# Adding the second key block's exponentials onto the first's on GpSimd, in the first attention of a four-stage kernel

## The reference, cut to what matters

```python
q = layernorm(x)                      # 16 heads of 32; keys and values are both ctx
scores = einsum('bhqd,bhkd->bhqk', q, k) * 32 ** -0.5   # causal: key <= query
exp_c  = exp(scores - rowmax(scores))
new_s  = exp_c.sum(axis=-1)
out    = einsum('bhqk,bhkd->bhqd', exp_c / new_s, v)
x      = x + tanh(g_xattn[0]) * out
```

## Time and profile before

| | |
|---|---|
| median of 3 runs | 1129.12 us (1126.06 to 1130.04) |
| profiled execution, its own time | 1127.54 us |
| its span, first to last instruction | 1125.5 us |
| PE / DVE / ACT / POOL busy, share of the span | 97% / 75% / 50% / 10% |
| POOL instructions | 212 |
| a turn of L0, PE start to PE start | 33.05 us |

### The profile page before, as it was taken

How to read it: one execution, slowest core, us unless ns; L and a number is a source line. 1 busy time by engine, 2 the same in 40 slices (tenths; PEclk the granted TensorE clock), 3 DMA queues, 4 the chain that set the end, 5 groups by cost and what they waited for, 6 DMA issues and landing times.

```text
span 1125.5 us, 25576 instructions
## 1 busy us (share of the span) xinstructions
PE 1092.2 (97%) x10386; PEld 662.7 (59%) x10386; DVE 839.0 (75%) x1437; ACT 567.1 (50%) x918; POOL 117.9 (10%) x212
## 2 busy tenths in 40 slices
PE   8899999999999999999999999899999999999998
PEld 3555555556777777777776655455554545454544
DVE  5788888778676657567566667887878788778786
ACT  4767666765433333333333353464554546372654
POOL 1101100110000000000001212020202030111010
PEclk9999999999999999999999999999999999999899
DMA  9565555433112011021010200101010101000001
GB/s 362 194 194 181 187 189 177 145 105 122 67 39 66 20 39 38 23 73 39 19 57 20 85 10 30 38 2 57 1 57 1 58 1 39 1 11 10 11 10 39
DMA packets 29267, 79.24 MB, mean 70 GB/s; under 512 B 3040, under 2 KB 3296, under 8 KB 28896
## 3 DMA queue, kind: packets, MB, share of 16 engines
q1 hardware_dynamic: 29152, 77.61, 21.0%
HBM read 65.02 MB, written 12.58 MB: 69 GB/s over the span
## 4 chain that ended last, share of the span: by engine, by line
PE 89%; DVE 4%; issue 3%; ACT 2%; POOL 1%; DMA 1%; SPq 0%; DVEq 0%; ACTq 0%; POOLq 0%
PE bank L693 10%; PE bank L589 10%; PE bank L590 10%; PE bank L675 10%; PE bank L551 9%; PE bank L798 8%; PE bank L431 5%; PE bank L828 5%; PE bank L786 5%; PE bank L748 3%; PE bank L767 2%; PE bank L456 2%; PE bank L516 2%; PE bank L483 2%; PE bank L504 2%
## 5 line engine op out<-in xcount | busy, mean ns | idle before, releaser
L589 PE MATMUL bank<-ARENA,W 128*128 128x256 f16 x1024 | 227.3, 273 | 0.7 <-issue 0.7
L590 PE MATMUL bank<-ARENA,W 128*128 128x256 f16 x1024 | 227.3, 273 | 0.0
L1006 ACT ACTIVATE ARENA<-bank 128x512 f32<-128x512 f32 (+3 forms) x143 | 92.9, 687 | 72.3 <-PE bank L431 35.5
L675 PE MATMUL bank<-W,ARENA 128*128 128x512 bf16 x512 | 120.8, 379 | 0.0
L551 PE MATMUL bank<-ARENA 128*128 128x512 f32 x256 | 117.7, 603 | 0.9 <-DMA ARENA<-in_wkv 0.9
L798 PE MATMUL bank<-W,ARENA 128*128 128x512 bf16 x512 | 117.7, 379 | 0.4 <-DVE W L1737 0.4
L693 PE MATMUL bank<-ARENA 128*128 128x512 f32 x256 | 116.9, 599 | 0.0
L589 PEld LDWEIGHTS bank<-ARENA,W 128*128 128x128 bf16 x1024 | 100.2, 98 | 19.1 <-issue 1.3
L590 PEld LDWEIGHTS bank<-ARENA,W 128*128 128x128 bf16 x1024 | 100.2, 98 | 18.0
L1006 ACT ACTIVATE ARENA<-ARENA 128x512 f16<-128x512 f32 x64 | 40.3, 630 | 133.3 <-DVE ARENA L1591 129.5
L1591 DVE SCALAR_TENSOR_TENSOR ARENA<-bank,ARENA 128x512 f32<-128x512 f32 x64 | 48.0, 750 | 72.3 <-PE bank L590 69.0
(11 more groups left out here) (181 smaller groups left out, 1799.6 us busy)
## 6 DMA issues: line engine op xcount, KB each, us to landing
W<-in_w SPq DMA_DIRECT2D x48, 512.0 KB, 4.3
ARENA<-in_w SPq DMA_DIRECT2D x24, 512.0 KB, 3.6
kv_store<-ARENA SPq DMA_DIRECT2D x32, 256.0 KB, 4.3
W<-kv_store SPq DMA_DIRECT2D x15, 512.0 KB, 4.1
ARENA<-in_ctxT SPq DMA_DIRECT2D x8, 512.0 KB, 3.9
X<-in_x SPq DMA_DIRECT2D x8, 512.0 KB, 5.7
ARENA<-in_ctx SPq DMA_DIRECT2D x8, 512.0 KB, 5.9
out<-X SPq DMA_DIRECT2D x16, 256.0 KB, 2.1
```

What stands on the lines that cost most here:

```text
L589: pe.matmul(bank[:, i * S:(i + 1) * S], W0[:, at:at + P], xt_half(b, 0)[:, k, :], start=(k == 0), stop=False)
L590: mm = pe.matmul(bank[:, i * S:(i + 1) * S], W0[:, at:at + P], xt_half(b, 1)[:, k, :], start=False, stop=(k == KD - 1))
L675: mm = pe.matmul(banks[6 + t], hx(q, what)[:, i * S + t * P:i * S + (t + 1) * P], W0[:, UP_AT + m * D:UP_AT + (m + 1) * D], start=(m == 0 ...
L1006: return act.activation(to, src, ACT.Copy)
```

## The change

GpSimd adds, for each group of four heads, the second key block's exponentials onto the columns of the first block that belong to the same queries (`a_add_probs`). The sums then need the first block alone, over 256 columns. The weighing keeps both blocks; since the first block's columns now hold p0 + p1, the second block is multiplied by v1 - v0, which GpSimd makes in place once per batch (`a_values_apart`): v0 (p0 + p1) + (v1 - v0) p1 = v0 p0 + v1 p1. Weigh and sum wait for these two through new semaphores `a_pa` and `a_dv`. For half 0 they are cut in two parts by head group, and the second parts stand behind scores(b,3).

```diff
-                pe.wait_ge((s.ld_rv0, s.ld_rv1)[b % 2], 16 * (b // 2 + 1))
-                pe.wait_ge(s.a_ex, 16 * b + 8 * half + 8)
-                for n in range(2):
+                if parts[0] == 0:
+                    pe.wait_ge(*ringA[4].freed(f"pv{half}", turn))
+                    pe.wait_ge(s.a_dv, b + 1)
+                for n in parts:
+                    pe.wait_ge(s.a_pa, 4 * b + 2 * half + n + 1)
...
-                for n in range(2):
-                    for kb in range(TB):
-                        at, q0 = kb * S, kb * P
-                        for j in range(4):
-                            mm = pe.matmul(part(total, j)[:, q0:S], bufA["count"][:, n, :], bufA["PT"][:, 4 * n + j, at:at + S - q0],
-                                           start=(kb == 0 and n == 0), stop=(kb == 1 and n == 1), skip_group_check=True)
-                mm.then_inc(s.a_sum, 1)
...
+                for n in parts:
+                    pe.wait_ge(s.a_pa, 4 * b + 2 * half + n + 1)
+                    for j in range(4):
+                        mm = pe.matmul(part(total, j)[:, 0:S], bufA["count"][:, n, :], bufA["PT"][:, 4 * n + j, 0:S],
+                                       start=(n == 0), stop=(n == 1), skip_group_check=True)
...
-                a_weigh(turn, b, 0)
+                a_weigh(turn, b, 0, (0,))
+                a_sum(turn, b, 0, (0,))
                 a_scores(b, 3)
-                a_sum(turn, b, 0)
+                a_weigh(turn, b, 0, (1,))
+                a_sum(turn, b, 0, (1,))
...
+            def a_values_apart(b):
+                near, far = (bufA["RV"][:, b % 2 * TB + kb, :] for kb in range(TB))
+                pool.wait_ge((s.ld_rv0, s.ld_rv1)[b % 2], 16 * (b // 2 + 1))
+                pool.tensor_tensor(far, far, near, ALU.subtract).then_inc(s.a_dv, 1)
+
+            def a_add_probs(b, g):
+                PT = bufA["PT"][:, g % 2 * 4:g % 2 * 4 + 4, :]
+                pool.wait_ge(s.a_ex, 16 * b + 4 * g + 4)
+                pool.tensor_tensor(PT[:, :, P:S], PT[:, :, P:S], PT[:, :, S:TRI], ALU.add).then_inc(s.a_pa, 1)
+
+            for f in range(NB + 1):
+                b = f - 1
...
+                if b >= 0:
+                    a_add_probs(b, 0)
+                if f < NB:
+                    a_add_bias(f, 0)
+                if b >= 0:
+                    a_add_probs(b, 1)
+                    a_add_probs(b, 2)
+                if f < NB:
+                    a_add_bias(f, 1)
+                if b >= 0:
+                    a_add_probs(b, 3)
+                if f < NB:
+                    a_values_apart(f)
```

More of the change, by code:

```diff
@@ L42 @@
     a_ve a_rstd a_xn a_xt a_xtr a_sc a_scr a_mhl a_mt a_mtr a_st a_ex a_pv a_pvr a_sum a_sumr a_ot a_otr a_xo
-    a_kb a_ab a_sg a_gs a_s a_r a_abs a_kv a_kvr
+    a_kb a_dv a_pa a_ab a_sg a_gs a_s a_r a_abs a_kv a_kvr
     b_ve b_rstd b_xn b_xt b_xh b_xl b_g b_gu b_sg b_h b_sq b_acc b_fold b_ss b_me b_inv b_hh b_hl b_pr b_xy b_neg b_w1
@@ L491, in a_probs, with a_weigh @@
                             mm.then_inc(s.a_st, 1)
-            def a_weigh(turn, b, half):
+            def a_weigh(turn, b, half, parts=(0, 1)):
                 RV = bufA["RV"][:, b % 2 * TB:(b % 2 + 1) * TB, :]
                 pv = banks[4]
-                pe.wait_ge(*ringA[4].freed(f"pv{half}", turn))
-                pe.wait_ge((s.ld_rv0, s.ld_rv1)[b % 2], 16 * (b // 2 + 1))
-                pe.wait_ge(s.a_ex, 16 * b + 8 * half + 8)
-                for n in range(2):
+                if parts[0] == 0:
[3 more added lines that the diff above has]
+                    pe.wait_ge(s.a_pa, 4 * b + 2 * half + n + 1)
                     for kb in range(TB):
@@ L505, in a_weigh, with a_sum @@
                                            start=(kb == 0), stop=(kb == 1), skip_group_check=True)
-                mm.then_inc(s.a_pv, 1)
-            def a_sum(turn, b, half):
+                if parts[-1] == 1:
+                    mm.then_inc(s.a_pv, 1)
+            def a_sum(turn, b, half, parts=(0, 1)):
                 total = banks[5]
-                pe.wait_ge(s.a_ex, 16 * b + 8 * half + 8)
-                pe.wait_ge(*ringA[5].freed(f"sum{half}", turn))
-                for n in range(2):
-                    for kb in range(TB):
-                        at, q0 = kb * S, kb * P
-                        for j in range(4):
-                            mm = pe.matmul(part(total, j)[:, q0:S], bufA["count"][:, n, :], bufA["PT"][:, 4 * n + j, at:at + S - q0],
-                                           start=(kb == 0 and n == 0), stop=(kb == 1 and n == 1), skip_group_check=True)
-                mm.then_inc(s.a_sum, 1)
+                if parts[0] == 0:
+                    pe.wait_ge(*ringA[5].freed(f"sum{half}", turn))
+                for n in parts:
[3 more added lines that the diff above has]
+                                       start=(n == 0), stop=(n == 1), skip_group_check=True)
+                if parts[-1] == 1:
+                    mm.then_inc(s.a_sum, 1)
             def a_turn_sums(turn, b):
@@ L2021, in a_add_bias @@
                 pool.tensor_tensor(kv, kv, keep["row"], ALU.add).then_inc(s.a_kb, 1)
[L2023 to L2027, removed]
+            def a_values_apart(b):
[9 more added lines that the diff above has]
+                if f < NB:
+                    pool.wait_ge(s.a_ve, f + 1)
+                    inverse_root(keep["rstd"], keep["ve"], TB).then_inc(s.a_rstd, 1)
+                else:
+                    pool.wait_ge(s.b_ve, 1)
+                    inverse_root(keep["rstd"], keep["ve"], TB).then_inc(s.b_rstd, 1)
+                if b >= 0:
[9 more added lines that the diff above has]
+                    a_add_probs(b, 3)
+                if f < NB:
+                    a_values_apart(f)
             def b_inverse(b):
@@ L2085, in pool_program @@
             for b in range(NB):
[L2086 to L2089, removed]
+                if b:
                     b_inverse(b - 1)
```

## The result

The changed kernel takes 1156.46 us (median of 4 runs, 1154.09 to 1160.54) against 1129.21 beside it: ratio 1.025, 95% interval 1.023 to 1.0269. It is slower by 27 us. The profiled execution took 1158.69 us, 31 more than the one before. The forecast was 1153, slower.

A forecast was written before the change was run, and what follows sets the result against it. TensorE's queue was taken to bound L0. Added 4.2 us for each of batches 1 to 4, 3.1 for batch 5, 2.0 for 6, 3 for 0, 1 for the last turn: 25.9 on 1127.5 gives 1153, range 1135 to 1168.

The forecast's parts named there:

- The saving: TensorE's sums in L0: dropping 128 products of 128 columns gives 0.43 us per half, at most 6.9 us.
- Length of the additions: GpSimd, each addition or subtraction of 512 elements per partition: 1.3 us, with 1.0 to 1.6 allowed.
- A meeting costs 1.0 us: VectorE in L0: a GpSimd addition meeting an instruction with SBUF inputs holds it up by 1.0 us.
- steps 1 to 5: One turn up to scores(b,3): GpSimd meetings delay VectorE, L1387 starts 2.85 us late and scores(b,3) 2.6 us late.
- Step 6: Turn after scores(b,3): late second weighing part, then ScalarE's copy, sign passes and query copies, put probs(b,2) 4.2 us late.
- Batch 1: L0's turn of batch 1: 4.2 us longer, the same as for each of batches 2 to 4.
- The clock: Rival: TensorE's idling before scores(b,3) and probs(b,2) lowers the granted clock, up to 1 us a turn, 1160; chance 0.1.
- The last turn: L0's last turn, without sign passes or queries behind the copy: 1 us longer.
- three signs of being wrong: VectorE's busy time per line unchanged, the wait before probs(b,2) absent, or TensorE waiting for GpSimd directly.
- Order only, without meetings: Rival: meetings cost nothing, only TensorE's order does, +0.85 us per turn, 6 us over 7 turns, 1134; chance 0.12.
- Faster by the saving: Rival: ScalarE's chain behind the copy has room, TensorE keeps 0.43 us per half, 1121; chance 0.03.
- Longer additions: Rival: GpSimd additions take 1.6 us and meetings 1.4, 1.5 to 2.5 us more per turn, 1165 to 1170; chance 0.12.

The follow-up runs named there:

- the last experiment: Changed kernel with 32 filling bfloat16 products on TensorE before scores(b,3) in batches 2, 3 and 4 alone: 1152.65 us, ratio 1.0215 to the kernel before.
- write-only kernel: Changed kernel with each GpSimd addition and subtraction replaced by a memset of the same elements: 1133.49 us, ratio 1.0044 to the kernel before.
- order-alone kernel: Kernel before with half 0's weighing and sums cut in two, second parts behind scores(b,3), no GpSimd additions: 1138.34 us, ratio 1.008.
- the additions beside: Kernel before with five float32 GpSimd additions per turn on data nobody reads, none in batch 7: 1139.51 us, ratio 1.0089.
- the two pairs above: Changed kernel with half 0's cut undone against kernel before with short sums only (1.0139, 0.9945); changed kernel against GpSimd memsets instead (1.025, 1.0044).

## Why the prediction was right, point by point

**The saving** was priced at 6.9 us and measured 6.2, with an interval of 3.8 to 8.7. A half's sums are 1.07 us long against 1.51, the 0.43 of the forecast.

**Length of the additions**, taken as 1.3 us: 1.27 us at the median for the new shape, and 1.46 for the subtraction. Lengths of 1.6 us and more, up to 1.76, occur only where an addition begins while VectorE is busy with a two-input instruction. GpSimd has the time, as said.

**A meeting costs 1.0 us.** The held-up instructions of the turn shown are 0.96, 1.09 and 1.04 us longer than their kind. The rule of the Trainium skill, SBUF — State Buffer, section Who interferes with whom, gives the right kind of instruction (two SBUF inputs against a reading GpSimd; a reduction is not touched; a GpSimd instruction that only writes does not hold up L1443). The trace bears out its "for the whole instruction" better than my 1.0 did. From the start of L1443, L1441 and L1452 the GpSimd instruction had 1.10, 1.22 and 1.18 us to go, and each grew by that less 0.13 or 0.14. A meeting thus costs nearly all that is left of the GpSimd instruction, 1.09 us at most in the ternary chain, and my 1.0 came close because these meetings begin early in it.

**The walk.** In steps 1 to 5 it put L1391's start at 16.4 us after the sums (13.51 + 2.85); it was 16.5. It gave 2.3 and 1.7 us for the two waits; they were 2.40 and 1.51. The steps behind them held: the root and the reciprocals late, project(f,0) waiting a little (0.3 us). Step 6 had probs(b,2) 4.2 us late; in the turn shown it starts 201.19 - 175.59 = 25.60 us after the sums against 20.17, 5.4 late. With the filling in three turns it is 24.54 after the sums, 4.4 late; the rest is the clock. With the clock held up, batches 2 to 4 take 37.4 us a turn, 4.4 more than before.

**The sum, by turns.** From sum to sum the profiles differ by 2.0, 6.0, 5.0 and 5.4 us for batches 1 to 4, and by 4.8 for 5 and 6 together; batch 0 accounts for 3.6 and the rest of L0 for 2.7. The forecast had 4.2 four times, 5.1, 3 and 1, in all 25.9; the measured are 29.4 in the profiled execution, and 27 by the medians. That the total is so near is in part luck: batch 1 was put too high by about as much as batches 2 and 3 were put too low. Three terms were mis-sized:

- *Batch 1*: 4.2 forecast, 2.0 measured. In this turn there is no output of an earlier batch to add; L1432 runs 16 times, the first at 106.5. VectorE is 1.3 us earlier and the wait before scores(b,3) does not arise. The same hand-written loop says so; I had walked one late turn and applied it to all.
- *The clock*: a rival with a chance of 0.1, at up to 1 us a turn. It came on top of the forecast's own mechanism in batches 2 to 4, not in its place; 3.5 us there by the last experiment, and more in the last turn. The runs of this kernel, which differ by 6 us, go along with it, though this was not tested by itself: the two at 1158.7 and 1160.5 have a mean granted clock of 0.985, the two at 1154 have 0.988 and 0.991. In batch 0 the clock also falls, at 44 to 48 us, where the kernel before keeps it; what part of the 3.6 us that is stays open.
- *The last turn*, 1 forecast, 3.2 measured from sum to sum and 2.7 to the end of L0. Most of it arises at its start. From the sums to probs(b,0) TensorE takes 285.98 to 290.07, 4.09 us against 2.82, with waits of 1.30 and 0.55 us for a late VectorE. Behind them the granted clock falls once more, and from probs(b,0) to the end of the projection it takes 6.73 us instead of 5.10. Two stretches of the table, columns as above:

```profile
290.00:292.00 2.00, 1.93 (x41) 1.40 (x42) 1.97 (x6) 0.06 (x1) 0.00 (x0) 0.58 0.00 0
292.00:294.00 2.00, 2.00 (x8) 1.01 (x5) 1.93 (x5) 1.86 (x5) 0.14 (x1) 0.57 0.00 0
```

One of my three signs of being wrong did occur here: TensorE waits for GpSimd directly, which I had costed at nothing for half 1. Scores and projection of a next batch, the cover, don't exist behind batch 7.

```profile
313.66 0.86 PE L505 MATMUL bank<-ARENA 128*32 128x256 f32 x16 [0.87 <-POOL ARENA L2035]
```

It costs little net. From the last product ahead of this half's weighing to the first one behind its sums it is 311.23 to 315.31, 4.08 us, against 3.91 before.

**The rivals.** Order only, without meetings, was forecast as 1134 and is nearly the write-only kernel, 1133.49; it did not happen because the meetings did. Faster by the saving was ruled out by the 0.17 us wait, and the order-alone kernel shows the wait grow to 1.6. Longer additions did not occur.

**How the parts add up.** By the ratios the saving, the order and the additions beside make -6.2, +9.0 and +10.0 us, each alone, 13 together; the change makes 28. The gap is not between the cut and the meetings: undoing the cut gains 12 us with the additions running, and making it costs 9.0 without them. It lies in the kernel with the additions beside, which puts GpSimd's work at 10 us where the two pairs above put it at 22 and 23. There the additions meet fewer and other instructions, no engine waits for their results, and TensorE has the long sums, which leave VectorE more time. What each of the three is worth was not tested. With 22 in place of 10 the parts make 25 of the 28 us, and the clock is of the size of the rest.

## What to carry to other kernels

An idle engine is not a free one: before GpSimd is given work that reads SBUF, look at what VectorE executes at those moments, and put the work where VectorE reads PSUM or reduces. When an instruction is moved behind another, read what the *consumer's* queue holds behind its wait; two sign passes between the copies cost more here (9.0 us) than the products saved (6.2). A stand-in for moved work has to meet the same instructions as the work itself, or it prices too low. The change did pay, by a quarter per cent, once three queues had been rearranged around it.

## What the runs showed of the hardware that I had not expected

Behind the wait of 2.4 us before scores(b,3) the granted clock fell to 1.2 GHz in the turns of batches 2, 3 and 4 (at 124, 158 and 196 us), although TensorE was busy 198.23 of 221.64 us, 89%, of this stretch. In the kernel with the additions beside it, with waits of up to 1.7 us, it did not fall in those turns. But the length of one wait does not decide it: with the cut undone it fell in the turns of batches 3 and 4, where TensorE had waited 0.7 us and, after one part of the weighing, 1.3 and 1.5 us.

The strided addition, four rows of 128 elements that lie 384 apart, takes as long as the flat one of 512: 1.27 us both.
